# Decoder block on one core: the dt tile of a scan step projected a step earlier, its ScalarE and GpSimd parts moved to other units

## The reference

```python
zxbcdt = x @ in_proj_w.T                      # z, x, B, C and 128 rows of dt
dt = softplus(dt_in @ dt_proj_w.T + dt_proj_b)
dA = exp(dt[..., None] * A)                   # A: 1024 channels x 16 states
dBx = dt * x_full * Bg
h = dA_i * h + dBx_i                          # scan over 512 tokens
y = einsum('bgn,bgcn->bgc', C_i, h) + D_skip * x_full
y = (y * silu(z)) @ out_proj_w.T
```

## Time and profile before

| | |
|---|---|
| median of three runs | 2798.21 us |
| the profiled execution | 2799.06 us |
| its span | 2797.3 us |
| mean granted TensorE clock | 0.960 |
| PE busy | 2618.7 us (94%) |
| DVE busy | 2082.0 us (74%) |
| POOL busy | 1285.8 us (46%) |
| ACT busy | 1191.1 us (43%) |

### The profile page before, as it was taken

How to read it: one execution, slowest core, us unless ns; L and a number is a source line. 1 busy time by engine, 2 the same in 40 slices (tenths; PEclk the granted TensorE clock), 3 DMA queues, 4 the chain that set the end, 5 groups by cost and what they waited for, 6 DMA issues and landing times.

```text
span 2797.3 us, 32656 instructions
## 1 busy us (share of the span) xinstructions
PE 2618.7 (94%) x11152; PEld 1877.7 (67%) x11160; DVE 2082.0 (74%) x2656; ACT 1191.1 (43%) x1786; POOL 1285.8 (46%) x868
## 2 busy tenths in 40 slices
PE   7888888898889879999999999999999999999999
PEld 4443444454345337888888778788878788888887
DVE  5999899999999976543376677777877865555553
ACT  5655555555555635422254543343333422222221
POOL 4899899899999961210001023123222422222220
PEclk9999899899899879999999999999999999999999
DMA  7754655555465437121111112112111121111111
GB/s 248 220 165 129 180 150 139 166 158 148 125 182 160 132 113 266 54 76 53 62 51 61 40 44 69 46 46 68 46 39 46 45 53 46 51 48 50 49 46 68
DMA packets 152311, 275.37 MB, mean 98 GB/s; under 512 B 27344, under 2 KB 27856, under 8 KB 151632
## 3 DMA queue, kind: packets, MB, share of 16 engines
q1 hardware_dynamic: 152144, 273.27, 32.7%
HBM read 178.01 MB, written 61.34 MB: 86 GB/s over the span
## 4 chain that ended last, share of the span: by engine, by line
PE 66%; DVE 9%; issue 8%; POOL 8%; ACT 4%; DMA 3%; SPq 1%; POOLq 0%; DVEq 0%; ACTq 0%
PE ps L1757 19%; PE ps L1759 19%; PE ps L1758 19%; DVE state L1401 4%; POOL read L1233 4%; PE ps L1806 3%; PE ps L1822 3%; ACT ps L896 1%; DMA vpack<-vl 1%; DMA b_d<-ev 1%; PE ps L1966 1%; POOL dt_t L1197 1%; POOL sp_rest L1182 1%; PE ps L1940 1%; DMA uraw<-y_d 1%
## 5 line engine op out<-in xcount | busy, mean ns | idle before, releaser
L1233 POOL TENSOR_TENSOR read<-state,c_t 128x512 f32<-128x512 f32 x512 | 662.9, 1316 | 74.4 <-DVE state L1401 35.8
L1401 DVE TENSOR_TENSOR_SCAN state<-ps,drive 128x512 f32<-128x512 f32 x512 | 622.5, 1216 | 4.2 <-ACT ps L896 1.7
L1295 POOL TENSOR_TENSOR wdeq<-packed,scales 128x1024 f32<-128x1024 f16 x96 | 256.2, 2668 | 800.7 <-DVE packed L1530 800.7
L1757 PE MATMUL ps<-xh,ghi 128*128 128x512 f32 x1536 | 607.3, 395 | 0.0
L1759 PE MATMUL ps<-xh,glo 128*128 128x512 f32 x1536 | 598.0, 389 | 0.0
L1758 PE MATMUL ps<-xl,ghi 128*128 128x512 f32 x1536 | 597.8, 389 | 0.0
L896 ACT ACTIVATE ps<-ps,a_exp 128x512 f32<-128x512 f32 x512 | 337.2, 661 | 385.4 <-PE ps L1806 383.9
L1392 DVE TENSOR_TENSOR drive<-ps,b_t 128x512 f32<-128x512 f32 x512 | 344.2, 672 | 53.6 <-PE ps L1806 49.5
L1697 DVE TENSOR_TENSOR act_o<-act_o,ps 128x512 f32<-128x512 f32 x192 | 131.8, 686 | 284.6 <-PE ps L1759 283.2
L1153 ACT ACTIVATE ahi<-act_o 128x512 fp32r<-128x512 f32 x192 | 121.6, 633 | 520.6 <-DVE act_o L1697 520.6
L1757 PEld LDWEIGHTS ps<-xh,ghi 128*128 128x128 f32 x1536 | 288.4, 188 | 62.6 <-issue 3.1
(11 more groups left out here) (197 smaller groups left out, 3842.0 us busy)
## 6 DMA issues: line engine op xcount, KB each, us to landing
whi<-w_d SPq DMA_DIRECT2D x63, 256.0 KB, 4.9
wlo<-w_d SPq DMA_DIRECT2D x63, 256.0 KB, 5.5
b_d<-ev SPq DMA_DIRECT2D x32, 256.0 KB
dpack<-dh SPq DMA_DIRECT2D x64, 128.0 KB, 4.4
dpack<-dl SPq DMA_DIRECT2D x64, 128.0 KB, 2.3
b_t<-b_d SPq DMA_DIRECT2D x32, 256.0 KB, 5.4
vpack<-vh SPq DMA_DIRECT2D x64, 128.0 KB, 2.3
vpack<-vl SPq DMA_DIRECT2D x64, 128.0 KB, 2.4
```

Of the source, the lines that this page charges most:

```text
L1233: pool.tensor_tensor(read[:, n % RRING, :], state[:, n % SRING, :], c_t[:, g % 2, :], ALU.mult).then_inc(read_ready, 1)
L1295: pool.tensor_tensor(wdeq[:, :].rearrange("p (h n) -> p h n", h=2), codes, scale, ALU.mult).then_inc(deq, 1)
L1401: dve.tensor_tensor_scan(state[:, n % SRING, :], ps[:, decay_bank(n), :], drive[:, n % DRING, :], 0.0, ALU.mult, ALU.add)\
L1757: pe.matmul(out_, w_h, x_h, start=(start and k == 0), stop=False)
```

## The change

A step q is called late if q % 8 == 0 or q <= 4; the other 24 are early ones. For the late steps everything stays where it was. For an early step:

- `dt_project(q)` runs in unit 0 of step q - 2, ahead of that unit's projection, not in unit 11.
- The five `soft_...` operations of ACT run in units 3 to 7 of step q - 2, not 12 to 15.
- POOL's `soft_rest`, `soft_sum`, `soft_dt`, `dt_x` run in units 8, 10, 12, 14 of step q - 2, not in 0 to 3 of step q - 1.
- `dt_high`, `v_high` run in units 0 and 2 of step q - 1 (before 6 and 8), `dt_low`, `v_low` in units 1 and 4 (before 7 and 9).
- SP loads the packed tiles right after C (and x), ahead of the store of y, of both later weight loads and of the step's three spills; with a late next step its order is the old one.

The dt tile's bank is 6 for all q >= 4. The jobs' banks are now 5, 6, 5 in each step (from job 12 on), so the second job of the step follows the dt tile in bank 6 and waits for `soft_pos` of it. `load_x` waits for a gather instead of for y.

```diff
+        def late(q):
+            return q % CT == 0 or q <= 4
+
         def dt_bank(q):
...
+            return 7 if q < 4 else 6
+
+        def job_bank(job):
+            return 5 + job % 2 if job < 12 else 5 + job % IN_TILES % 3 % 2
...
         def dt_ahead(job):
             nb, k = divmod(job, IN_TILES)
             g = CT * nb - 2 + k // 3
-            return max([0] + [q + 1 for q in range(4, g + 2) if dt_bank(q) == 5 + job % 2])
+            if job < 12 or job_bank(job) == 5 or g < 3:
+                return 0
+            return g + 2 if late(g + 2) else g + 3
...
                 if q >= 3:
-                    sp.wait_ge(y_ready, q - 2)
+                    sp.wait_ge(gathered, 4 * (q - 3) + 1)
...
                 if jobs:
                     weights_after(first)
+                if jobs and late(g + 1):
                     spill(first)
                 if 0 <= g + 1 < STEPS:
                     load_c(g + 1)
+                if g + 2 < STEPS and not late(g + 2):
+                    load_x(g + 2)
+                if g + 1 < STEPS and not late(g + 1):
+                    load_pack_dt(g + 1)
+                    load_pack_v(g + 1)
+                if jobs and not late(g + 1):
+                    spill(first)
                 if g >= 1:
                     store_y(g - 1)
                 if jobs:
                     weights_after(first + 1)
-                if 0 <= g + 1 < STEPS:
+                if g + 1 < STEPS and late(g + 1):
                     load_pack_dt(g + 1)
                     load_pack_v(g + 1)
                 if jobs:
                     spill(first + 1)
-                if g + 2 < STEPS:
+                if g + 2 < STEPS and late(g + 2):
                     load_x(g + 2)
...
-                        if c == 6:
+                        if c == (6 if late(g + 1) else 0):
                             dt_high(g + 1)
-                        if c == 8:
+                        if c == (8 if late(g + 1) else 2):
                             v_high(g + 1)
-                    if nb < B:
+                    if nb < B and late(g + 2):
...
+                    elif nb < B:
+                        if c == 3:
+                            soft_abs(g + 2)
+                        if c == 4:
+                            soft_pos(g + 2)
+                        if c == 5:
+                            soft_exp(g + 2)
+                        if c == 6:
+                            soft_one(g + 2)
+                        if c == 7:
                             soft_log(g + 2)
...
+                    elif g + 1 < STEPS:
+                        if c == 1:
+                            dt_low(g + 1)
+                        if c == 4:
+                            v_low(g + 1)
+                    if g + 2 < STEPS and not late(g + 2):
+                        if c == 8:
+                            soft_rest(g + 2)
+                        if c == 10:
+                            soft_sum(g + 2)
+                        if c == 12:
+                            soft_dt(g + 2)
+                        if c == 14:
+                            dt_x(g + 2)
...
+                    if nb < B and not late(g + 2) and c == 0:
+                        dt_project(g + 2)
                     if jobs and (c < 12 or g < 2):
                         project(first + c // 4, c % 4)
-                    if nb < B and c == (10 if g < 2 else 11):
+                    if nb < B and late(g + 2) and c == (10 if g < 2 else 11):
                         dt_project(g + 2)
```

More of the change, by code:

```diff
@@ L374, in last_in_bank, with job_ahead, job_ahead_of_dt @@
             return m
+        def late(q):
+            return q % CT == 0 or q <= 4
         def dt_bank(q):
-            if q < 4:
-                return 7
-            nb, k, jobs = step_jobs(q - 2)
[L381 to L387, removed]
+            return 7 if q < 4 else 6
+        def job_bank(job):
+            return 5 + job % 2 if job < 12 else 5 + job % IN_TILES % 3 % 2
+        def job_ahead(job):
+            m = job - 1
+            while m >= 0 and job_bank(m) != job_bank(job):
+                m -= 1
+            return m
+        def job_ahead_of_dt(q):
+            nb, k, jobs = step_jobs(q - 2)
+            job = first_job(q - 2) + 2 * late(q) if jobs else IN_TILES * (nb + 1)
+            return job_ahead(job) if job_bank(job) == 6 else max(
+                j for j in range(job) if job_bank(j) == 6)
         def dt_ahead(job):
@@ L819, in take @@
                 act.wait_ge(job_done, job + 1)
-                bank = ps[:, 5 + job % 2, :]
+                bank = ps[:, job_bank(job), :]
                 if tile == 0:
@@ L979, in _ @@
                             soft_one(g + 2)
+                            soft_log(g + 2)
+                    elif nb < B:
[8 more added lines that the diff above has]
+                        if c == 7:
                             soft_log(g + 2)
@@ L1252, in _ @@
                         out_weights_low(2 * (g - STEPS + 3) + (c - 12) // 2)
-                    if g + 1 < STEPS:
+                    if g + 1 < STEPS and late(g + 1):
                         if c == 0:
@@ L1381, in dt_split @@
                 dve.wait_ge(dthi_ready, nb + 1)
-                dve.tensor_tensor(dtlo[:, :], ps[:, 5 + (IN_TILES * nb) % 2, :],
+                dve.tensor_tensor(dtlo[:, :], ps[:, job_bank(IN_TILES * nb), :],
                                   dthi[:, :].bitcast(F32), ALU.subtract).then_inc(dtlo_ready, 1)
@@ L1771, in project @@
                         pe.wait_ge(w_loaded[s], 32 * ((job - IN_TILES) // 3 + 1))
-                    if job >= 2:
-                        if (job - 2) % IN_TILES == 0:
-                            pe.wait_ge(dtlo_ready, nb + 1)
+                    if job_ahead(job) >= 0:
+                        if job_ahead(job) % IN_TILES == 0:
+                            pe.wait_ge(dtlo_ready, job_ahead(job) // IN_TILES + 1)
                         else:
-                            pe.wait_ge(job_taken, taken_count(job - 2))
+                            pe.wait_ge(job_taken, taken_count(job_ahead(job)))
                     if dt_ahead(job):
@@ L1780, in project @@
                     pe.wait_ge(ln_lo, FT * nb + f + 1)
-                mm = three_pass(ps[:, 5 + job % 2, :], [(whi[s][:, f, :], wlo[s][:, f, :],
+                mm = three_pass(ps[:, job_bank(job), :], [(whi[s][:, f, :], wlo[s][:, f, :],
                                                         xh[nb][:, f, :], xl[nb][:, f, :])],
@@ L1794, in dt_project @@
                 if q >= 4:
-                    job = last_job(dt_bank(q), q)
+                    job = job_ahead_of_dt(q)
                     if job % IN_TILES == 0:
```

## The result

The changed kernel takes 2836.97 us (median of four runs, 2832.77 to 2839.21), beside 2796.85 us for the kernel before: ratio 1.0141, 95% interval 1.0122 to 1.0160. That is 40 us slower. In a second comparison it took 2834.94 us against 2799.4, ratio 1.0133 (1.0116 to 1.0149), 36 us. The forecast was 2819 with a range of 2798 to 2838: the direction and the range hold. The size, 21 us, was little more than half of the measured one, and the loss lies above the 10 to 30 us to which the forecast gave its 0.64. The first profiled execution took 2832.77 us, the fastest of its four, 33.7 us above the one before; its scan stage, from the first scan to the last, grew by 31.0 us.

What follows compares the result with a forecast made beforehand. DVE, nearly full in the scan stage, was taken to bound it, its drives waiting for PE's spread of v. Terms 18 - 12 + 17 - 2 = +21 us on 2799.06 gave 2820, median 2819; range 2798 to 2838.

Steps and rivals of the forecast that it cites:

- rival 3: Unit 10 of steps 7, 15, 23: weights stay late through another transfer; +33 us, 2831, chance 0.12.
- part E: Ordinary early steps, unit 4: `soft_pos` ends about when PE's projection would start; taken as nothing, up to 6 us.
- A: Unit 0 of 24 steps: three added matmuls delay the spread for unit 2; +18 us, bounds 12 and 31.
- C: Steps 3, 7, 15, 23: `soft_pos` waits for `soft_dt`, delaying unit 6's drive; +17 us, bounds 6 and 24.
- B: Unit 10 of steps 7, 15, 23: SP's new order removes the weight waits; -12 us, bounds 0 and -12.5.
- D: Unit 0 of step 5: packed tiles come early, so the wait for them goes; -2 us, bounds 0 and -2.5.
- Rival 1: Start of steps: clock stays high across units 15 and 0, waits at unit 2 go; -21 us, 2777, chance 0.12.
- Rivals 2, 3 and 4: Rival 2: `soft_dt` in time for unit 4, 2802, chance 0.12; rival 4: early steps' chain no earlier, 2816, within 0.64.

Runs made afterwards that it cites:

- c_pos2: The changed kernel with a second buffer for sp_pos, so soft_pos(g + 2) no longer waits for soft_dt(g + 1): 2817.82 us, ratio 1.0060 to the kernel before.
- ac_both: The changed kernel with a second buffer for sp_pos and the dt projection of early steps in unit 2: 2805.63 us, ratio 1.0025 to the kernel before.
- warm_c: The changed kernel with a second sp_pos buffer and three unread products in each of units 12 to 15 of most steps 5 to 27: 2793.53 us, ratio 0.9985.
- warm_unit1: Changed kernel with second sp_pos buffer, unread PE products, POOL's parts in units 8 to 11, dt projection in unit 1, ACT's in units 2 to 6: 2781.63 us.

## Why the prediction was right, and where it was off

The direction and three of the four terms were right for the reasons given. That the range held owes something to luck: its upper end, 2838, is the price of rival 3 with part E, neither of which came, and the measured 2836.97 is 1 us inside it. What brought it there instead is A, 6 us larger than the sum had it, C, 2 us larger, and the rest told below.

- **What bounds the stage, DVE's drives waiting for PE:** right. Waits went up by some 24 us in the first profile and the scan stage by 31.0.
- **A, +18 (bounds 12 to 31):** right in kind, too small. The waits at unit 2 rose by 24.4 us. Two steps were off. "I take 0.8 for a step" was too small: the 24 steps with the added matmuls wait 22.1 us more, 0.92 a step, where the sum had 18. And I had worked out where the half clock ends from the old rows and left it there. It starts as before, in the idle units, but lasts longer: of steps 3 to 29, 12 began in a half clock stretch of 6.8 us or more before, and 19 after. So steps 6, 14 and 22, with no dt projection in unit 0, also wait more (0.81, 0 and 0.85 us before, 1.33, 1.31 and 1.32 after), the other 2.3 us. Why the long stretch is now met so often was not settled.
- **B, -12:** right. The three waits are gone in the changed kernel, and the order alone gave 12.0 us at unit 10. Not foreseen: A and B are not independent. On the kernel before, A alone costs 6.6 us in total, since B's wait absorbs a part. The B stores went 4.4 us earlier in their step, not 5.6, which was still enough.
- **C, +17 (4 x 4.2):** right, link by link; 19.4 us at unit 6 measured, and c_pos2 takes 19 us off the total. Expected for step 15 was a wait of 4.2 us, it is 5.11: the half clock covered all matmuls behind the pause, where I had counted seven tenths.
- **D, -2:** right, the wait at unit 0 of step 5 is gone. **E, 0 (up to 6):** 0 in the changed kernel; 5.8 us at unit 6 once the projection stands in unit 2 (ac_both).
- **What the sum lacked:** DVE's operations on SBUF alone, 5.9 us, and in the other direction 6 us at unit 10 in steps without projections. The first is the step "POOL's parts, spread out, leave POOL less behind, but no scan waits for a read now, so nothing": true of the scans, but not of the other operations of DVE. So the sum of the named terms was 21, and with measured sizes it is 24.4 + 19.4 - 12.5 - 2 = 29. The two that were missing cancel; some 2 us are smaller ones, and that makes the 31 of the scan stage. The rest of the 36 to 40 us is the spread of executions and some 2 us after the scan stage.
- **Rival 1, the dip goes:** the Trainium skill, "TensorE: Matmul & The Clock Gate", Part 1, has activity release the clock. By that rule, more matmuls in unit 0 could have helped. They did not: they came after the clock had fallen, and it was 0.50 from 413.43 to 420.26 with them in. Where added matmuls stand in the idle stretch itself the trace agrees with the rule: warm_c has 1.00 at this place. **Rivals 2, 3 and 4** did not come: `soft_dt` ended no earlier, the weights were in time, and the chain was early, as its packed tiles show.

## To carry to other kernels

Before moving work to an emptier place, ask what stands behind it in that engine's queue and at which clock it runs there: three matmuls were free in unit 11 and cost 0.9 us a step in unit 0, ahead of the one spread that DVE waits for. Where a regular schedule meets an irregular one, look for shared one-buffer tiles: four such meetings cost 19 us here, the 24 ordinary steps 22. And a wait removed can uncover one that it had hidden, so terms of a sum on one path are to be checked against each other.

## What the hardware showed that I had not expected

**VectorE and GpSimd wait for each other where VectorE has both inputs in SBUF.** DVE's scaling of x in unit 13 of step 10 (both large inputs in SBUF) beside POOL's timeline. Before, POOL had caught up and was idle when it asked:

```profile
402.32 0.72 DVE L1365 SCALAR_TENSOR_TENSOR xlr<-xlr,rms,selraw 128x512 f32<-128x512 f32 x1
...
400.77 1.28 POOL L1233 TENSOR_TENSOR read<-state,c_t 128x512 f32<-128x512 f32 x1 [0.37 <-DVE state L1401]
402.48 1.70 POOL L1233 TENSOR_TENSOR read<-state,c_t 128x512 f32<-128x512 f32 x1 [0.43 <-DVE state L1401]
```

After, a part of the dt chain had just started there:

```profile
412.31 1.78 DVE L1410 SCALAR_TENSOR_TENSOR xlr<-xlr,rms,selraw 128x512 f32<-128x512 f32 x1
...
412.29 1.26 POOL L1228 TENSOR_TENSOR dt_t<-sp_log,sp_pos 128x512 f32<-128x512 f32 x1
413.51 1.71 POOL L1264 TENSOR_TENSOR read<-state,c_t 128x512 f32<-128x512 f32 x1
```

DVE ends 0.5 us after POOL's operation ended (414.09 and 413.55), and POOL's next takes 1.7 us instead of 1.28 (before, the read that began while DVE was at work took 1.70 too). The Trainium skill, "SBUF — State Buffer", section "Who interferes with whom", says that a VectorE instruction with two SBUF inputs contends with a GpSimd one that reads SBUF and that the later one blocks. These rows agree, and so do the others of the stage. It has 40 DVE operations with both inputs in SBUF. In the changed kernel 33 of them began while POOL was at work, and each ended 0.54 to 0.56 us after the POOL operation that it had met, however long that made it (0.67 to 1.78 us). The seven that found POOL idle took 0.67 to 0.73 us. In the kernel before, 31 met POOL at work and ended 0.54 to 0.60 us behind it, and nine found it idle. So the 5.9 us more in "other" are waits for POOL. An operation with one input in PSUM did not wait, though POOL was reading all the while (before, step 6):

```profile
267.40 0.67 DVE L1382 TENSOR_TENSOR dtlo<-ps,dthi 128x512 fp32r<-128x512 f32 x1
...
266.84 2.53 POOL L1233 TENSOR_TENSOR read<-state,c_t 128x512 f32<-128x512 f32 x2
```

With PE at full clock one of the 40 waited through five POOL operations in a row, four of the reads below and the one behind them (warm_unit1, step 10):

```profile
369.09 5.98 DVE L1413 SCALAR_TENSOR_TENSOR xlr<-xlr,rms,selraw 128x512 f32<-128x512 f32 x1
...
367.08 6.21 POOL L1267 TENSOR_TENSOR read<-state,c_t 128x512 f32<-128x512 f32 x5
373.26 1.25 POOL L1244 TENSOR_TENSOR dl<-dt_t,dh 128x512 fp32r<-128x512 f32 x1
```

That is not one operation's wait. What lets POOL keep the SBUF for several operations here, when DVE gets in after one elsewhere, stays open; moving the scaling did not tell it. It costs some 4 us in each of two steps of the fastest kernel (4.86 and 5.16 us instead of 0.72), which would be the next thing to look at.

**Matmuls whose result nobody reads made the kernel faster.** With three more in each of the units 12 to 15, PE executes 294 matmuls more in the scan stage (3461 against 3167) and the stage is 25 us shorter than without them (966.5 against 991.2, warm_c against c_pos2), and the granted clock in the stage rises from 0.88 to 0.94. The waits at unit 2 that went, 31.6 us, cover it and the 7 us more in "other":

```profile
55.00:1023.00 968.00, 858.27 (x3461) 473.88 (x3459) 934.27 (x1067) 553.83 (x939) 907.29 (x710) 0.94 0.54 155
```
